# Folding query and key weights over a block diagonal, with the small weights' copies and the first maxima moved in the start of an attention kernel

## The chip, the cores and the metric

The kernel runs on one core of a Trainium2 chip. The metric is the device time of one execution in microseconds (us), the median of several runs. Engines are named as in the profile: PE (TensorE, matmuls; PEld its weight loads), ACT (ScalarE), DVE (VectorE), POOL (GpSimd), SP (the queue that issues DMAs). Each engine works through its own list of instructions strictly in the written order, and the lists meet only at semaphores.

## What is computed

For eight sequences of 1024 tokens and width 256, a layer norm feeds causal attention with 16 heads over a shared latent of 64, and a chain of three square weights with a tanh; both are added to the input.

```
xn      = layernorm(x)                         # x: 8 x 1024 x 256
q       = xn @ Wq                              # 16 heads of 64
latent  = xn @ Wkv_down                        # 64 wide, shared by all heads
k, v    = latent @ Wk_up, latent @ Wv_up
attn    = softmax(causal(q k^T / sqrt(64)))
y       = (attn @ v) @ Wout
ff      = tanh(xn @ weight @ aux1 @ aux2 + bias)
out     = x + y + ff
```

Since `k` is `latent @ Wk_up`, the kernel multiplies per head `Wq` by the transpose of `Wk_up` once ("folds" them) and never builds `k`; it does the same with `Wv_up` and `Wout`, and with the three square weights.

## The kernel before

**Staging.** The program is one plan, a list of named items, and each engine's program walks that list and emits its own part of each item. The list has two parts. `first_plan` is written out by hand: constants, layer norm of the first sequence, the turning (transposing) and folding of all weights, the first keys and queries, and the maxima of the first unit. `body_plan` comes from a planner (class `Order`) with its own table of costs; it holds the whole attention loop of 8 sequences and doesn't read `first_plan`. In the hand-written part the order of the tuple list is the order on every engine, so moving an item moves it in the queues of all engines that have a part in it.

**Items of the first part.** `LN0`, `LN1`, `LN4` are the layer norm on DVE; `T` transposes `x` on PE (L1121) into `xT_hi` (ACT, L1250) and its residue `xT_lo` (item `TL`, DVE, L1416). `W` items are the work on weights (functions `fold_on_pe`, `fold_on_act`, `fold_on_dve`): "turn wq" and "turn wk" transpose `Wq` and `Wk_up` (PE L814) and ACT copies the results to SBUF (L869); "fold wqk 0" and "fold wqk 1" multiply them for one half of the 256 input rows each (PE L839), ACT writes the rounded part `wqk_hi` (L869) and DVE the residue `wqk_lo` (L930). "turn others" transposes `Wv_up`, `aux1` and `weight` (L814); "fold aux" and "fold wff" are products of square weights (L796), "fold wvo" and the end of "fold wff" fold the values with `Wout` (L805), and "split wvo" is the DVE's residues of these (L936, L941). `K0`, `K` make the keys' latent and `Q0`, `Q` the folded queries (both L969, three products per result); `KN` turns the latent (L1143). After `Q`, ACT writes `q_hi` in two instructions and `q_lo` in one (L1269, L1274), SP copies halves of `q_hi` by two DMAs (L1477, L1479), and DVE makes the residue (`QL`, L1427), of which `QD` copies a part by DMA (L1487). `MAX` is a product whose row maxima DVE takes (L1062, L1299). `MT` turns the eight maxima of a unit (L1075), ACT copies them, and a DMA puts them in a row of `q_lo`, which the first score product `ST` (L1026, L1029) waits for. A DVE maximum of the body is L1304.

**Order and waits.** In a product the PE program waits for its inputs and for its PSUM bank to be left (`bank_left`): of the eight banks the `P0` items (`T`, `K`, `KN`, `Q`) take 6, 0 and 1 in turn, and the maxima take 2, 3 and 4. The compiler emits each fp32 product as two passes, so the 16 products of one "fold wqk" show as 32 matmuls in the trace; transposes and products of rounded (fp32r) operands are one pass each. In "fold wqk" a product takes one head: the stationary operand is 64 rows of `wqT` and the moving one 64 columns of `wkT`. The heads of a pair lie in the upper and the lower 64 rows.

**Loads.** SP issues all loads at the start in the order `x` (two halves), `Wq`, `Wk_up`, `Wkv_down`, `Wv_up` and the rest.

## Time and profile before

| | |
|---|---|
| median of 3 runs | 1976.43 us (1972.88 to 1980.48) |
| profiled execution, device time | 1977.45 us |
| its span, first to last instruction | 1975.7 us |
| mean granted PE clock | 0.994 |
| busy: PE, DVE, POOL, ACT | 99%, 69%, 73%, 58% of the span |
| first score product (L1026) starts | 55.18 us |

The profile is of one execution on its one core. Of the 1975.7 us the hand-written part takes the first 55, and the planner's body the rest. The chain that ended last is 89% PE; the largest shares of it are the products of the attention loop (L1044 23%, L969 21%, L1062 14%). To read the start, the timeline is of more use than the shares: it lists runs of equal instructions with their start and how long they lasted together. The granted clock (PEclk) is a share of full speed, with 1.00 for 2.4 GHz and 0.50 for 1.2 GHz.

### The profile page before, as it was taken

The page shows a single profiled execution, that of the slowest core. Times are in us where ns is not written, and L with a number is a line of the kernel's source. Part 1 is how long each engine was busy: PE and PEld are TensorE (multiplying, and loading weights), DVE is VectorE, ACT ScalarE, POOL GpSimd, SP SyncE. Part 2 cuts the span into 40 slices and gives each one's busy share as a digit, 9 for nine tenths or more (in the row PEclk, how much of TensorE's full clock was granted, in tenths as well). Part 3 has the DMA queues.
Part 4 walks back from the last instruction along what each step waited for, and adds up shares of the span by engine and source line. Part 5 has one row for each costly group of instructions (what it writes and reads, how often), then busy time and mean ns, then how long its engine had stood idle before and what let it go on. Part 6 is the DMA issues. An engine that isn't in the chain of part 4 may idle for free.

```text
span 1975.7 us, 38820 instructions
## 1 busy us (share of the span) xinstructions
PE 1948.6 (99%) x13568; PEld 1322.7 (67%) x13568; DVE 1372.7 (69%) x3623; ACT 1148.9 (58%) x2203; POOL 1450.7 (73%) x1276
## 2 busy tenths in 40 slices
PE   9999999999999999999999999999999999999997
PEld 7666666667666666766666666766676766766754
DVE  4778666786577867677676875868667786676642
ACT  4565565565566665656565565555665655655652
POOL 0577678886877867877778876877768777787882
PEclk8999999999999999999999999999999999999999
DMA  3222121212222212122122222122221221212210
GB/s 111 71 66 57 47 61 47 80 52 52 55 60 76 63 42 60 52 80 53 44 62 62 71 61 52 45 62 67 60 70 48 75 51 47 66 49 55 60 42 20
DMA packets 117599, 116.50 MB, mean 59 GB/s; under 512 B 24092, under 2 KB 100764, under 8 KB 117404
## 3 DMA queue, kind: packets, MB, share of 16 engines
q1 hardware_dynamic: 117404, 114.02, 21.7%
q8 instruction: 108, 1.77, 0.4%
q14 instruction: 87, 0.71, 0.1%
HBM read 53.67 MB, written 8.91 MB: 32 GB/s over the span
## 4 chain that ended last, share of the span: by engine, by line
PE 89%; DVE 4%; issue 3%; ACT 2%; POOL 1%; DMA 1%; POOLq 0%; ACTq 0%; SPq 0%; DVEq 0%
PE ps L1044 23%; PE ps L969 21%; PE ps L1062 14%; PE ps L1026 13%; PE ps L1029 12%; PE ps L1089 3%; DVE split_lo L1339 2%; POOL p_sum L1464 1%; PE ps L1075 1%; PE ps L1121 1%; DMA q_hi<-q_hi 1%; ACT probs L1199 1%; PE ps L839 0%; ACT q_hi L1269 0%; PE ps L1002 0%
## 5 line engine op out<-in xcount | busy, mean ns | idle before, releaser
L1464 POOL TENSOR_TENSOR p_sum<-p_sum,probs 128x512 f32<-128x512 f32 x660 | 845.9, 1309 | 132.0 <-ACT probs L1199 130.7
L1199 ACT ACTIVATE probs<-ps 128x512 f32<-128x512 f32 x1152 | 662.9, 598 | 308.6 <-PE ps L1029 292.2
L1299 DVE CUSTOM_DVE_ANT_0 ps<-ps,causal 128x512 f32<-128x512 f32 (+4 forms) x1024 | 520.1, 527 | 228.8 <-PE ps L1062 221.8
L1044 PE MATMUL ps<-probs,latent 128*32 128x512 f32 x4608 | 516.2, 594 | 0.0
L1062 PE MATMUL ps<-k_hilo,q_hi 128*128 128x512 f32 (+4 forms) x1536 | 471.3, 356 | 3.7 <-DMA q_hi<-q_hi 1.7
L1026 PE MATMUL ps<-q_hi,k_hilo 128*128 128x512 f32 x1152 | 470.1, 408 | 4.9 <-DVE wff_lo L936 1.9
L1029 PE MATMUL ps<-q_lo,k_ones 65*128 65x512 f32 x1152 | 457.1, 397 | 0.0
L1304 DVE TENSOR_REDUCE maxima<-ps 128x1 f32<-128x512 f32 (+1 forms) x512 | 326.2, 637 | 165.0 <-PE ps L1062 161.4
L1464 POOL TENSOR_TENSOR p_sum<-probs 128x512 f32<-128x512 f32 x222 | 288.7, 1318 | 128.2 <-ACT probs L1199 122.9
L1044 PEld LDWEIGHTS ps<-probs,latent 128*32 128x32 f32 x4608 | 139.7, 110 | 316.9 <-issue 312.2
L1062 PEld LDWEIGHTS ps<-k_hilo,q_hi 128*128 128x128 f32 x1536 | 279.3, 189 | 100.2 <-issue 25.5
L1450 POOL TENSOR_SCALAR_AFFINE_SELECT probs<-probs 128x512 f32<-128x512 f32 x256 | 166.8, 667 | 211.8 <-ACT probs L1199 211.2
L1026 PEld LDWEIGHTS ps<-q_hi,k_hilo 128*128 128x128 f32 x1152 | 217.9, 189 | 58.6 <-ACT probs L1199 28.5
L1029 PEld LDWEIGHTS ps<-q_lo,k_ones 65*128 65x128 f32 x1152 | 217.9, 189 | 18.1
L1208 ACT ACTIVATE y<-ps 128x512 f32<-128x512 f32 x128 | 76.5, 598 | 261.0 <-PE ps L1044 260.5
L1339 DVE TENSOR_TENSOR split_lo<-y,split_hi 128x512 fp32r<-128x512 f32 x127 | 171.1, 1348 | 49.0 <-ACT split_hi L1236 48.2
L1439 POOL TENSOR_TENSOR y<-y,norm 128x512 f32<-128x512 f32 x127 | 163.5, 1290 | 29.9 <-DMA norm<-recips 29.9
L1269 ACT ACTIVATE q_hi<-ps 64x512 fp32r<-64x512 f32 x256 | 151.6, 592 | 48.3 <-PE ps L969 45.4
L969 PE MATMUL ps<-wvo_hi,split_hi 128*128 128x256 f32 x512 | 150.1, 293 | 8.7 <-DVE split_lo L1339 7.6
L969 PE MATMUL ps<-xT_hi,wqk_hi 128*128 128x256 f32 x512 | 145.8, 285 | 0.0
L969 PE MATMUL ps<-wvo_lo,split_hi 128*128 128x256 f32 x512 | 145.3, 284 | 0.0
L969 PE MATMUL ps<-wvo_hi,split_lo 128*128 128x256 f32 x512 | 145.2, 284 | 0.0
(108 smaller groups left out, 2270.8 us busy)
## 6 DMA issues: line engine op xcount, KB each, us to landing
q_hi<-q_hi SPq DMA_DIRECT2D x256, 128.0 KB, 2.4
norm<-recips SPq DMA_DIRECT2D x254, 128.0 KB, 3.0
q_lo<-q_lo SPq DMA_DIRECT2D x128, 128.0 KB, 2.4
x_in<-in_L_attn_x_bld SPq DMA_DIRECT2D x16, 512.0 KB, 5.0
acc<-in_L_attn_x_bld SPq DMA_DIRECT2D x32, 256.0 KB, 3.1
out_x<-acc SPq DMA_DIRECT2D x64, 128.0 KB, 1.7
q_lo<-rows SPq DMA_DIRECT2D x128, 4.0 KB
rows<-norm SPq DMA_DIRECT2D x127, 4.0 KB
```

The lines of the kernel that those rows point to most:

```text
L969: last = nc.tensor.matmul(dst, weights(a, c), moving(b, c), start=(c == 0 and n == 0), stop=(c == of - 1 and n == 2))
L1026: nc.tensor.matmul(bank, k_hilo[par][:, blk], q_hi[buf][:, g:OCTET:2, columns(unit)], start=True, stop=False)
L1029: nc.tensor.matmul(bank, k_ones[par][:, blk], q_lo[buf][0:LATENT + 1, g:OCTET:2, columns(unit)], start=False, stop=True).then_inc(st_full, 1)
L1044: last = nc.tensor.matmul(y_bank[row:row + WIDTH, :], latent[par][:, key_block(unit, s), half:half + WIDTH], probs[:, t % PT_SLOTS, g * BA ...
L1062: nc.tensor.matmul(bank[:, 0:w], q_hi[half % Q_BUFS][:, h, columns(unit)], k_hilo[par][:, k0:k0 + w], start=True, stop=True).then_inc(max_ ...
L1199: nc.scalar.activation(probs[:, t % PT_SLOTS, g * BANK:(g + 1) * BANK], ps[:, bank_of[kind, key], :], ACT.Exp).then_inc(exp_done, 1)
L1299: nc.vector.tensor_tensor_reduce(bank, bank, causal[:, BANK - w:BANK], 1.0, LOWEST, ALU.add, ALU.max, maxima[:, unit % 4, h, 0:1]).then_in ...
L1304: nc.vector.tensor_reduce(maxima[:, unit % 4, h, 1:2], bank, AX.X, ALU.max).then_inc(max_free, 1)
L1339: nc.vector.tensor_tensor(split_lo[:, slot, :], y[:, key % Y_SLOTS, :], split_hi[:, slot, :].bitcast(F32), ALU.subtract).then_inc(norm_lo, 1)
L1439: nc.gpsimd.tensor_tensor(y[:, slot, :], y[:, slot, :], norm[:, slot, :], ALU.mult).then_inc(y_normal, 1)
L1450: nc.gpsimd.affine_select(out=v, in_=v, pattern=[[0, 4], [1, P]], compare_op=ALU.is_ge, fill=0.0, base=0, channel_multiplier=-1).then_inc( ...
L1464: nc.gpsimd.tensor_tensor(sums, other, probs[:, slot, part], ALU.add).then_inc(pool_done, 1)
```

## The change

Five things change, all of them in the hand-written first part.

1. "turn wk" comes ahead of "turn wq", and `Wk_up` is loaded ahead of `Wq`. ACT copies the turned key weights in two instructions of 64 rows into `wk_pairs`, in which a pair of heads is a 128x128 block with its two 64x64 blocks on the diagonal. POOL zeroes that tile first (an eighth constant), and ACT waits for it.
2. "fold wqk" takes a pair of heads in one product: 128 rows of `wqT` against the 128 columns of a block. It is 8 products of 128 columns instead of 16 of 64 in each item. In the first item PE waits for the copies of `wqT` bank by bank.
3. The copies of "turn others" go from ACT to DVE; `weight` is turned into bank 2 instead of 1, and with that the wait for bank 1 goes.
4. `KN` and the second `QL` and `QD` move behind "turn others", and the maxima stand ahead of and between the foldings in another split (2, 3 and 3, with banks 4, 3, 2 in turn).
5. `MT` comes ahead of the next queries, and "split wvo" right behind it.

```
-    plan += [("LN4", (0, k)) for k in range(2)] + [("W", "turn wq"), ("W", "turn wk")]
+    plan += [("LN4", (0, k)) for k in range(2)] + [("W", "turn wk"), ("W", "turn wq")]
...
-    plan += [*two_parts("Q", (0, 0)), ("QL", (0, 0)), *two_parts("Q", (0, 1)), ("KN", 0), ("QD", (0, 0))]
+    plan += [*two_parts("Q", (0, 0)), ("QL", (0, 0)), *two_parts("Q", (0, 1)), ("QD", (0, 0))]
...
-    plan += [("W", "turn others"), ("W", "fold aux"), *maxima[:2], ("QL", (0, 1)), ("QD", (0, 1)), maxima[2]]
-    plan += [("W", "fold wvo"), *maxima[3:6], ("W", "fold wff"), *maxima[6:]]
-    plan += [("Q0", (1, 0)), ("MT", 0), ("Q", (1, 0)), *two_parts("Q", (1, 1))]
+    plan += [("W", "turn others"), ("KN", 0), ("QL", (0, 1)), ("QD", (0, 1)), *maxima[:2]]
+    plan += [("W", "fold aux"), *maxima[2:5], ("W", "fold wvo"), *maxima[5:], ("W", "fold wff")]
+    plan += [("MT", 0), ("W", "split wvo"), *two_parts("Q", (1, 0)), *two_parts("Q", (1, 1))]
     plan += [("QL", (1, 0)), ("QD", (1, 0)), ("XA", 0), ("XA", 1), ("XA", 2)]
-    plan += [("W", "split wvo"), ("QL", (1, 1)), ("QD", (1, 1))]
+    plan += [("QL", (1, 1)), ("QD", (1, 1))]
...
-            bank[kind, key] = 2 + n_max % 3
+            bank[kind, key] = 4 - n_max % 3
...
-        wkT = acc_flat[:, 0:512].rearrange("p (j n) -> p j n", n=LATENT)
+
+        wk_pairs = probs[:, 8, :].rearrange("p (j n) -> p j n", n=2 * LATENT)
...
+                (wk_in, Wk_up.rearrange("c h k -> c (h k)"), wk_loaded),
                 (wq_in, Wq.rearrange("(c p) h k -> p c (h k)", p=P), wq_loaded),
-                (wk_in, Wk_up.rearrange("c h k -> c (h k)"), wk_loaded),
...
+            nc.gpsimd.memset(probs[:, 8, :], 0.0).then_inc(consts_made, 1)
...
-                for g in range(2):
-                    r = g * HD
-                    for j in range(HEADS // 2):
-                        last = nc.tensor.matmul(
-                            wq_banks[2 * c + g][:, j * LATENT:(j + 1) * LATENT],
-                            wqT[r:r + HD, j, c * P:(c + 1) * P], wkT[r:r + HD, j, :],
-                            start=True, stop=True)
-                    last.then_inc(w_full, 1)
+                for j in range(HEADS // 2):
+                    if c == 0 and j % 2 == 0:
+                        pe.wait_ge(w_copied, 3 + j // 2)
+                    last = nc.tensor.matmul(wq_banks[2 * c + j // 4][:, j % 4 * P:(j % 4 + 1) * P],
+                                            wqT[:, j, c * P:(c + 1) * P], wk_pairs[:, j, :],
+                                            start=True, stop=True)
+                    if j % 4 == 3:
+                        last.then_inc(w_full, 1)
             elif what == "turn others":
-                bank_left(1)
...
-                for bank, w in ((7, aux1_in), (1, w_in)):
+                for bank, w in ((7, aux1_in), (2, w_in)):
...
-                pe.wait_ge(w_copied, 12)
+                pe.wait_ge(w_turned, 3)
...
-                copied(5, acc_flat[:, 0:512], wk_bank)
+                act.wait_ge(consts_made, 8)
+                pairs = wk_bank.rearrange("p (j n) -> p j n", n=LATENT)
+                for g in range(2):
+                    rows = slice(g * HD, (g + 1) * HD)
+                    copied(1, wk_pairs[rows, :, g * LATENT:(g + 1) * LATENT], pairs[rows, :, :])
...
-            elif what == "turn others":
-                copied(10, acc_flat[:, 512:1024], ps[:, 5, :])
-                copied(11, norm[:, 0, :], ps[:, 7, :])
-                copied(12, acc_flat[:, 1536:2048], ps[:, 1, :])
...
+            elif what == "turn others":
+                for n, (dst, bank) in enumerate(((acc_flat[:, 512:1024], 5), (norm[:, 0, :], 7),
+                                                 (acc_flat[:, 1536:2048], 2))):
+                    dve.wait_ge(w_full, 10 + n)
+                    nc.vector.tensor_copy(dst, ps[:, bank, :]).then_inc(w_turned, 1)
```

What that makes of the engines' lists is shown at three places; names are the program's buffers, sizes are those of the moving operand or the output, and a line number of the changed kernel is a few higher for the same statement. The brackets name the semaphores waited for ahead of an instruction.

ACT at its start, before: the table load, the copies of the turned weights (`probs<-ps`), of `x` (`xT_hi`) and of the folded weights (`wqk_hi`).

```order
L869 ACT_TABLE_LOAD
L869 ACTIVATE probs<-ps 128x512 [waits w_full] x5
L1250 ACTIVATE xT_hi<-ps 128x512 [waits p0_full] x2
L869 ACTIVATE wqk_hi<-ps 128x8x64 [waits w_full] x2
L1250 ACTIVATE xT_hi<-ps 128x512 [waits p0_full] x2
```

ACT at the same place with the change.

```order
L872 ACT_TABLE_LOAD [waits w_full]
L872 ACTIVATE probs<-ps 64x8x64 [waits consts_made]
L872 ACTIVATE probs<-ps 64x8x64 [waits w_full]
L872 ACTIVATE probs<-ps 128x512 [waits w_full] x4
L1257 ACTIVATE xT_hi<-ps 128x512 [waits p0_full] x2
L872 ACTIVATE wqk_hi<-ps 128x512 [waits w_full] x2
```

The two half-height copies of the key weights stand ahead of the four of `wqT`, and the table load, which carried no wait before, stands behind a wait for the first turned weights (`w_full`).

PE from the end of the first queries to the second fold of the values, before: `k_hilo` with `ident` is `KN`, `p_sum` and `y` are the small weights to be turned, `y,norm` is "fold aux", `k_hilo,q_hi` a maximum's product and `probs` of 64x256 "fold wvo".

```order
L1143 MATMUL ps<-ident,k_hilo 128x64 [waits p0_free]
L1143 MATMUL ps<-ident,k_hilo 128x64 x7
L814 MATMUL ps<-ident,p_sum 128x64 [waits others_loaded,kn_copied]
L814 MATMUL ps<-ident,p_sum 128x64 x7
L814 MATMUL ps<-ident,y 128x128 x8
L796 MATMUL ps<-y,norm 128x256 [waits p0_free,w_copied]
L796 MATMUL ps<-y,norm 128x256 x3
L1062 MATMUL ps<-k_hilo,q_hi 128x512 [waits q_twice0_0]
L1062 MATMUL ps<-k_hilo,q_hi 128x512 x2
L805 MATMUL ps<-probs 64x256 [waits w_copied]
L805 MATMUL ps<-probs 64x256 x11
L1062 MATMUL ps<-k_hilo,q_hi 128x512 [waits max_free]
```

PE at the same place with the change.

```order
L817 MATMUL ps<-ident,p_sum 128x64 [waits others_loaded]
L817 MATMUL ps<-ident,p_sum 128x64 x7
L817 MATMUL ps<-ident,y 128x128 x8
L1150 MATMUL ps<-ident,k_hilo 128x64 [waits p0_free]
L1150 MATMUL ps<-ident,k_hilo 128x64 x7
L1069 MATMUL ps<-k_hilo,q_hi 128x512 [waits q_twice0_0]
L1069 MATMUL ps<-k_hilo,q_hi 128x512
L799 MATMUL ps<-y,norm 128x256 [waits p0_free,w_turned]
L799 MATMUL ps<-y,norm 128x256 x3
L1069 MATMUL ps<-k_hilo,q_hi 128x512
L1069 MATMUL ps<-k_hilo,q_hi 128x512 [waits max_free]
L1069 MATMUL ps<-k_hilo,q_hi 128x512 [waits max_free,q_twice0_1]
```

`KN` has moved behind the turning, whose wait for `kn_copied` is gone; two maxima stand ahead of "fold aux", which waits for `w_turned` in place of `w_copied`.

DVE ahead of the first score product, before: maxima (`ISA`), the residue of the next queries (`q_lo`), then the residues of the folded weights.

```order
L1299 ISA ps,maxima<-ps,causal 128x512 [waits max_full]
L1299 ISA maxima 128x1
L1427 TENSOR_TENSOR q_lo<-ps,q_lo 128x2x256 [waits p0_hi]
L936 TENSOR_TENSOR wff_lo<-ps,wff_hi 128x512 [waits w_copied]
L941 TENSOR_TENSOR wvo_lo<-ps,wvo_hi 128x512 [waits w_copied]
L941 TENSOR_TENSOR wvo_lo<-ps,wvo_hi 128x512 x3
L1427 TENSOR_TENSOR q_lo<-ps,q_lo 128x2x256 [waits p0_hi]
L1304 TENSOR_REDUCE maxima<-ps 128x1 [waits max_full]
```

DVE at the same place with the change.

```order
L1306 ISA ps,maxima<-ps,causal 128x512 [waits max_full]
L1306 ISA maxima 128x1
L943 TENSOR_TENSOR wff_lo<-ps,wff_hi 128x512 [waits w_copied]
L948 TENSOR_TENSOR wvo_lo<-ps,wvo_hi 128x512 [waits w_copied]
L948 TENSOR_TENSOR wvo_lo<-ps,wvo_hi 128x512 x3
L1434 TENSOR_TENSOR q_lo<-ps,q_lo 128x2x256 [waits p0_hi] x2
L1311 TENSOR_REDUCE maxima<-ps 128x1 [waits max_full]
L1306 ISA ps,maxima<-ps,causal 128x320 [waits max_full]
```

Both residues of the next queries now stand behind the five of the folded weights.

## Rows read from the trace of the kernel before

**Rows 1.** Busy time by stretch of the span; columns as in the answer's first line.
```profile
core 0: us, PE busy (x) PEld busy (x) DVE busy (x) ACT busy (x) POOL busy (x), PEclk, DMA share, GB/s
0.00:13.50 13.50, 11.69 (x48) 7.55 (x48) 9.77 (x42) 4.09 (x7) 1.93 (x11) 1.00 0.88 264
13.50:17.70 4.20, 4.20 (x40) 4.12 (x40) 3.10 (x9) 2.14 (x5) 0.00 (x0) 0.97 0.84 264
17.70:27.60 9.90, 9.90 (x43) 8.77 (x42) 3.28 (x5) 2.48 (x5) 0.00 (x0) 0.50 0.00 0
27.60:34.50 6.90, 5.04 (x38) 4.70 (x36) 2.08 (x3) 5.87 (x11) 0.00 (x0) 0.99 0.16 38
34.50:41.30 6.80, 6.09 (x23) 5.02 (x24) 0.00 (x0) 1.79 (x3) 0.00 (x0) 0.50 0.25 58
...
100.00:1900.00 1800.00, 1792.77 (x12566) 1219.38 (x12565) 1289.23 (x3398) 1070.92 (x2058) 1384.78 (x1208) 1.00 0.22 59
```

**Rows 2.** Timeline, 0 to 20 us: start us, us, engine, line, what.
```profile
0.80 1.28 ACT L869 ACT_TABLE_LOAD   x1 [0.80 <-PEq L1592]
...
9.51 1.91 PE L814 MATMUL ps<-ident,probs 128*128 128x128 f32 x16
...
10.14 2.56 ACT L869 ACTIVATE probs<-ps 128x512 f32<-128x512 f32 x5 [8.06 <-PE ps L814]
...
11.35 0.71 PE L814 MATMUL ps<-ident,p_sum 64*128 64x64 f32 x8
...
12.49 1.09 PE L1121 MATMUL ps<-ident,x_in 128*128 128x128 f32 x8 [0.43 <-DVE x_in L1404]
...
13.51 3.39 PE L839 MATMUL ps<-probs 64*128 64x64 f32 x32
13.88 1.29 DVE L1416 TENSOR_TENSOR xT_lo<-ps,xT_hi 128x512 fp32r<-128x512 f32 x2 [0.15 <-ACT xT_hi L1250]
...
15.47 0.49 DVE L923 TENSOR_TENSOR wkv_lo<-norm,wkv_hi 128x128 fp32r<-128x128 f32 x2
...
18.21 6.29 PE L839 MATMUL ps<-probs 64*128 64x64 f32 x32
```

**Rows 3.** Timeline, 24 to 33 us.
```profile
24.43 0.79 PE L969 MATMUL ps<-xT_hi,wkv_hi 128*128 128x512 f32 x1
...
28.32 0.40 PE L969 MATMUL ps<-xT_lo,wkv_hi 128*128 128x512 f32 x1
...
28.78 0.28 PE L969 MATMUL ps<-xT_hi,wqk_hi 128*128 128x256 f32 x1
...
31.66 0.98 PE L1143 MATMUL ps<-ident,k_hilo 128*128 128x64 f32 x8
...
32.38 0.62 SPq L1479 DMA_DIRECT2D q_hi<-q_hi  x1
```

**Rows 4.** Chain that ended last, in time order, 38 to 58 us.
```profile
38.22 3.51 PE ps L796 x8
41.73 0.68 PE ps L1062 x3
42.42 2.81 PE ps L805 x24
...
46.12 1.73 PE ps L796 x8
...
50.87 0.27 PE ps L1075
...
57.42 0.60 DVE q_lo L1427
```

**Rows 5.** Timeline, 51 to 56 us.
```profile
51.89 1.20 ACT L1269 ACTIVATE q_hi<-ps 64x512 fp32r<-64x512 f32 x2 [0.45 <-PE ps L969]
...
54.81 0.60 ACT L1274 ACTIVATE q_lo<-ps 128x512 fp32r<-128x512 f32 x1
```

**Rows 6.** DMA issues of the first 60 us: KB each, us to landing.
```profile
probs<-in_L_attn_Wq SPq DMA_DIRECT2D x1, 1024.0 KB, 7.5
...
q_hi<-q_hi SPq DMA_DIRECT2D x8, 128.0 KB, 2.4
```

More of the change, by code:

```diff
@@ L670, in build @@
         w_split = sem("w_split")
+        w_turned = sem("w_turned")
         x_loaded = [sem(f"x_loaded{i}") for i in range(2)]
@@ L823, in fold_on_pe @@
             elif what == "turn wq":
-                pe.wait_ge(consts_made, 7)
                 pe.wait_ge(wq_loaded, 16)
@@ L829, in fold_on_pe @@
             elif what == "turn wk":
+                pe.wait_ge(consts_made, 7)
                 pe.wait_ge(wk_loaded, 16)
@@ L832, in fold_on_pe @@
             elif what in ("fold wqk 0", "fold wqk 1"):
-                pe.wait_ge(w_copied, 5)
                 c = int(what[-1])
-                for g in range(2):
-                    r = g * HD
-                    for j in range(HEADS // 2):
-                        last = nc.tensor.matmul(
-                            wq_banks[2 * c + g][:, j * LATENT:(j + 1) * LATENT],
-                            wqT[r:r + HD, j, c * P:(c + 1) * P], wkT[r:r + HD, j, :],
-                            start=True, stop=True)
-                    last.then_inc(w_full, 1)
+                for j in range(HEADS // 2):
[6 more added lines that the diff above has]
+                        last.then_inc(w_full, 1)
             elif what == "turn others":
-                bank_left(1)
                 pe.wait_ge(others_loaded, 96)
                 transposes(ps[:, 5, :], [wv_in[:, j * P:(j + 1) * P] for j in range(HEADS // 2)])
-                for bank, w in ((7, aux1_in), (1, w_in)):
+                for bank, w in ((7, aux1_in), (2, w_in)):
                     transposes(ps[:, bank, :], [w[:, c, k * P:(k + 1) * P]
@@ L855, in fold_on_pe @@
             elif what == "fold wvo":
-                pe.wait_ge(w_copied, 13)
                 for n, bank in enumerate((5, 7, 6)):
+                    if bank == 6:
+                        pe.wait_ge(w_copied, 11)
                     wvo_bank(bank, n)
@@ L862, in fold_on_pe @@
                 square(0, wT, aux12)
+                bank_left(1)
                 wvo_bank(1, 3)
@@ L873, in fold_on_act @@
                 for n in range(4):
-                    copied(n + 1, wqT_flat[:, n * BANK:(n + 1) * BANK], wq_banks[n])
+                    copied(n + 2, wqT_flat[:, n * BANK:(n + 1) * BANK], wq_banks[n])
             elif what == "turn wk":
-                copied(5, acc_flat[:, 0:512], wk_bank)
+                act.wait_ge(consts_made, 8)
[3 more added lines that the diff above has]
+                    copied(1, wk_pairs[rows, :, g * LATENT:(g + 1) * LATENT], pairs[rows, :, :])
             elif what in ("fold wqk 0", "fold wqk 1"):
@@ L894, in wqk_part @@
         def wqk_part(w, n):
-            return (w[:, n // 2, :].rearrange("p (j g n) -> p j g n", g=2, n=LATENT)
-                    [:, :, n % 2, :], wq_banks[n].rearrange("p (j n) -> p j n", n=LATENT))
+            return w[:, n // 2, n % 2 * BANK:(n % 2 + 1) * BANK], wq_banks[n]
         def wvo_part(w, n):
@@ L928, in fold_on_dve @@
                     lo, bank = wqk_part(wqk_lo, n)
-                    dve.wait_ge(w_copied, 6 + n)
+                    dve.wait_ge(w_copied, 7 + n)
                     nc.vector.scalar_tensor_tensor(
@@ L933, in fold_on_dve @@
                         op1=ALU.subtract).then_inc(w_split, 1)
+            elif what == "turn others":
[3 more added lines that the diff above has]
+                    nc.vector.tensor_copy(dst, ps[:, bank, :]).then_inc(w_turned, 1)
             elif what == "split wvo":
-                dve.wait_ge(w_copied, 17)
+                dve.wait_ge(w_copied, 15)
                 nc.vector.tensor_tensor(wff_lo[:, :, :].rearrange("p c n -> p (c n)"), ps[:, 0, :],
@@ L938, in fold_on_dve @@
                                         ALU.subtract).then_inc(w_split, 1)
-                dve.wait_ge(w_copied, 18)
+                dve.wait_ge(w_copied, 16)
                 for n, bank in ((3, 1), (0, 5), (1, 7), (2, 6)):
```

## The prediction

> **What bounds the kernel now.** I read the busy time by stretch first. From 100 to 1900 us PE is busy for 1792.77 of 1800 us at full clock [rows 1], so the body is one queue of PE work, and what comes late into it comes out late by as much. The body's lists are the same in both kernels. So the question is how much earlier the start hands over. In the start I then read clock and idle time by stretch: PE stands at half clock from 17.7 to 27.6 and from 34.5 to 41.3 us, and idles for 1.9 of the 6.9 us between them [rows 1]. Then the timeline, for what each step waits for: the first transposes of x come at 12.49 behind DVE's normalization; the two foldings take 3.39 us at full and 6.29 us at half clock [rows 2]; the keys begin at 24.43 [rows 3]. Last the chain in order of time: fold aux 3.51 us, the other foldings and the maxima one behind another, MT at 50.87, and DVE's residue of the second next queries ending at 58.02 [rows 4]. That last end is my finish line, since the body's maxima queue behind it on DVE and PE needs their banks; behind it PE has no more long gaps.
>
> **The start up to the keys.** The clock and the warm-up are as before. PE turns the key weights at 9.5 in 0.7 us, then Wq in 1.9 us, to 12.1 [rows 2]. Wq landed 7.5 us after its issue, at 9.3 [rows 6]. It is now issued one DMA later (some 0.6 us, as the issue in [rows 3]) behind 0.25 MB, which at the 264 GB/s of the stretch is 1.0 us [rows 1], so it lands between 9.9 and 10.3. x's transposes still start at 12.5, at worst 12.7.
>
> ACT has a new cost. Before, the table load ran at 0.80 for 1.28 us while ACT had nothing to do [rows 2]. In the changed list it stands behind the wait for the first turned weights. It now runs from 10.3 to 11.6. Then come six copies instead of five at a pitch of 0.49 us (2.56 us for five, the last lasting 0.60) [rows 2], to 14.7, and the two of x to 15.2 and 15.7. DVE's residue of x, at 13.88 before, starts at 15.3. From there DVE has two residues (1.3 us), the casts and their residues (0.8 us, from the end of the first two to 15.96), two of the folded weights and two more of x, each about 0.65: 4.7 us, to 20.1 [rows 2]. The keys wait for the last of these and start at 20.2.
>
> Here the Trainium skill's page "ScalarE: Activation LUTs", section "What ACT_TABLE_LOAD costs", speaks against the change: it puts a load at about 1.28 us and a drain of some 1.38 us behind it. The row agrees with the first figure and can't show the second, as nothing followed. With 2.66 us the keys would start at 21.5, and the gain below would be 12.2 us, an estimate from that page.
>
> On PE a pair product is two passes with 128 columns moving and a 128x128 load. None such is in the trace. From below, the transposes of the same size run at 0.12 us each (1.91 for 16); from above, two-pass products with 256 columns (fold wff, 1.73 for 8) take 0.22 [rows 2, 4]. I take 0.12, as the columns streamed are the transposes'. Each folding is then 16 x 0.12 = 1.9 us: 13.6 to 15.5, x's other transposes to 16.5, the second folding to 18.4. The four waits of the first folding cost nothing: the copies end at 13.2, 13.7, 14.2 and 14.7, each before its pair is due. So PE is done at 18.4 and DVE sets the keys' start: 20.2 against 24.43, a gain of 4.2 us. POOL's added memset I cost at nothing: all of POOL's eleven instructions at the start take 1.93 us [rows 1], and even one as long as these together would end before ACT needs the tile at 11.6.
>
> **The clock.** The granted clock fell to 0.50 after the narrow foldings, whose passes have 64 rows loaded and 64 columns moving, and again after a stretch with 1.9 us of idle PE [rows 1, 2]. Both causes shrink: the new foldings load and stream twice as much per pass, and the idle time in the second place goes. I expect full clock throughout. The keys (12 x 0.23) and queries (24 x 0.12, both pitches from [rows 3]) then take 5.7 us instead of 7.2, to 25.9: a gain of 1.5 us.
>
> **From the queries to MT.** Before, PE waited after KN for ACT, which had six query copies and latent in front, turned at half clock, waited for ACT's copies, and folded aux at half clock. From 31.66 to 50.87 is 19.2 us [rows 3, 4]. Now the turning follows the queries directly: 0.7 for the values and 0.95 for eight of 128 columns, to 27.6; KN 1.0, to 28.5. The first two maxima need q_hi's DMAs: the first queries end at 24.5, ACT's two copies at 25.8, the second DMA is issued 0.7 later (as 32.38 is behind the first) and lands in 2.4 [rows 3, 6], at 29.0. So 0.5 us of wait; the two products take 0.5, to 29.5. Beside this DVE copies the three banks. Its copy of 128x512 is not in the trace; between 0.3 (half of a residue, which reads two operands) and 0.65 us I take 0.65, as the nearest row is its residues from PSUM [rows 2]. From 27.1 they end at 29.1, under the maxima; by the lower bound they end earlier and nothing is gained. Then PE works without a pause: fold aux 1.8, three maxima 0.7, fold wvo 2.8, three maxima 0.9, fold wff 1.75, its last bank 0.95 (a third of 2.81) [rows 4]. That is 8.9 us, and MT comes at 38.4. DVE's maxima, eight at 0.65 from 29.7, run inside the foldings; before, two of them stood alone ahead of MT. 12.5 us instead of 19.2: a gain of 6.7 us.
>
> **From MT to the body.** Before, 50.87 to 58.02, 7.15 us: DVE's five residues of the foldings stood between those of the two queries. Now they run from 38.4 to about 42, under the queries and their copies. PE's first half of the queries ends at 40.1, ACT's six copies take 3.5 (51.89 to 55.41) [rows 5], to 43.7, and the residue 0.7, to 44.4. MT's row needs ACT and a DMA, by q_hi's rows 0.7 to issue and 2.4 to land [rows 3, 6], so the first score products may start at 42.0 and don't set the end. 6.0 instead of 7.15: a gain of 1.15 us. What is late next is ACT, with the query copies.
>
> **The sum.** 4.2 + 1.5 + 6.7 + 1.15 = 13.6 us (58.02 to 44.4). Off the profiled execution's own 1977.45 us that is 1963.9. That execution is 1.0 above the median of the runs, so off the median it is 1962.8. I say 1963.0, 0.7% faster.
>
> **Rivals.**
> One half-clock stretch stays. PE's idle time of 1.8 us at 18.4 to 20.2 and the narrow work behind the queries speak for it. A stretch like that of 34.5 to 41.3, 6.8 us long, costs 3.4 us: a gain of 10.2 and 1966.2. Against it, the idle time lies between dense products, and the body, which has waits too, runs at 1.00 from 100 to 1900 us [rows 1]. The Trainium skill's "TensorE: Matmul & The Clock Gate", Part 4, says that transposes don't count as busy for the clock; 16 of them with KN and a wait behind would be such a place. Here the clock stayed at 1.00 through 9.5 to 13.5 us, which is nearly all transposes [rows 1, 2], so I give it 12%.
>
> Dear pair products. If a pass takes 0.22 as in fold wff, each folding takes 3.5 us, PE is the later one before the keys at 21.6, and the gain is 12.2: 1964.3. Against it, where load and stream are 128 each, as in the transposes, the load is hidden. 8%.
>
> The table load costs nothing. If it ran early or were hidden, DVE's residues of x would start at 13.9 as before and the keys at 18.7: a gain of 15.1 or 1961.3. Its place in the list speaks against it. 10%.
>
> The change does not do what it says: the start is shorter, and the body gives it back, since some later wait hangs on a transfer or a pace that the start does not move. About 1976. For it: PE's 7 us of idle time in the body. Against it: these are waits for other engines whose work moves with PE's. 7%.
>
> Slower. The clock, once half in the start, stays so into the body. From 20.2 to 44.4 us PE has about 20 us of work. At half clock all of it would add 20, less 13.6 gained: 1983. It decides from 13.6 us of full-clock work done at half, that is 27 us at half clock, against the 16.7 that the rows of before show in two pieces. With smaller mishaps of that sign, 4%.
>
> **How the numbers follow.** The forecast's own case has the rest, 59%. Unknown costs in it: the copies and the products' pace (up to 2 us lost), the table load's tail (1.4 lost), Wq's landing (0.2), better packing by 1 us, and the spread of before's runs, which is 4 us either way and 1 or 2 for a median. That is 1959 to 1968, and with the rivals near it 1958.5 to 1969 holds eight in ten. This kernel's measurement can tell about 0.5%, 9.9 us, from no change, which is at 1966.5. Faster by over that: 59 + 10 + 8 and half of the 12%, less a little for spread: 0.81. Within: 0.15. Slower: 0.04.
>
> **What would show it.** In the changed profile: ACT_TABLE_LOAD at about 10.3 for 1.28 us; each folding 16 passes in 1.9 us; DVE's residues of x as the releaser of the keys at 20.2; a granted clock of 1.00 from 13.5 to 44; no idle PE before the turning; MT near 38.4; the first score product near 42 against 55.18; and the body at its old pace, ending 13 to 14 us earlier. The prediction is wrong if the keys start after 22, if a half-clock stretch is left, or if a body event that came a given time after the first score product comes later after it now.

## The result and the profile after

The changed kernel takes 1964.13 us (median of 6 runs, 1960.96 to 1969.53) against 1978.45 for the kernel before in the same measurement (6 runs, 1972.88 to 1981.56). The medians are 14.3 us apart. The ratio is 0.994 with a 95% interval of 0.992 to 0.9959, which is 12 us of 1978 with an interval of 8 to 16: faster, clear of the noise. The profiled execution's span is 1962.0 us against 1975.7, 13.7 us less; 13.6 was forecast for this difference.

The busy time by stretch, for comparison with [rows 1]:

```profile
core 0: us, PE busy (x) PEld busy (x) DVE busy (x) ACT busy (x) POOL busy (x), PEclk, DMA share, GB/s
0.00:13.50 13.50, 10.84 (x42) 6.83 (x43) 9.66 (x40) 3.20 (x5) 2.83 (x12) 1.00 0.88 238
13.50:17.70 4.20, 4.20 (x40) 4.20 (x39) 3.32 (x11) 4.20 (x9) 0.00 (x0) 1.00 1.07 338
17.70:27.60 9.90, 8.73 (x67) 7.89 (x65) 6.05 (x11) 6.52 (x13) 0.00 (x0) 1.00 0.07 17
27.60:34.50 6.90, 6.40 (x44) 4.57 (x43) 5.21 (x13) 2.74 (x5) 0.00 (x0) 1.00 0.42 97
34.50:41.30 6.80, 6.80 (x47) 5.50 (x46) 5.02 (x11) 3.18 (x7) 0.00 (x0) 1.00 0.01 3
...
100.00:1900.00 1800.00, 1793.87 (x12578) 1220.00 (x12577) 1293.25 (x3391) 1073.06 (x2061) 1388.35 (x1212) 1.00 0.22 59
```

In 17.7 to 27.6 and 34.5 to 41.3 us, where PE stood at 0.50 before, it now runs at 1.00. The body is unchanged: PE is busy for 1793.87 of 1800 us against 1792.77. Measured from PE's restart behind the last residue of the queries (58.47 us before, 44.72 now; called the gate below) to the end of the span it lasts 1917.2 us before and 1917.3 now. In these two executions the start's 13.75 us arrive whole at the end. The line of the chain from which the gate before is read:

```profile
58.47 0.56 PE ps L1062 x2
```

That the two bodies agree to 0.1 us is chance, though. The experiments below have the same body, and in their profiled executions it lasts from 1914.2 us (MT as before) to 1921.4 us (zeros by ACT): from 100 to 500 us PE was busy for 399.20 us in the first of these and for 395.06 in the second. So a trace shows exactly what the start gains, but the time of one execution shows it only to within some 7 us.

The start's timeline, which answers to [rows 2] and the first row of [rows 3]:

```profile
2.85 0.95 POOL L790 MEMSET probs<- 128x1024 f32 x1
2.93 0.91 DVE L911 CAST ident<-norm 128x64 fp32r<-128x64 f32 x1 [2.93 <-POOL causal L786]
...
10.24 1.28 ACT L872 ACT_TABLE_LOAD   x1 [10.24 <-PE ps L817]
...
11.44 1.97 PE L817 MATMUL ps<-ident,probs 128*128 128x128 f32 x16 [1.28 <-DMA probs<-in_L_attn_Wq]
11.54 3.31 ACT L872 ACTIVATE probs<-ps 64x512 f32<-64x512 f32 x6
...
13.28 1.09 PE L1128 MATMUL ps<-ident,x_in 128*128 128x128 f32 x8
...
14.21 1.95 PE L841 MATMUL ps<-probs 128*128 128x128 f32 x16
...
15.36 1.29 DVE L1423 TENSOR_TENSOR xT_lo<-ps,xT_hi 128x512 fp32r<-128x512 f32 x2 [0.84 <-ACT xT_hi L1257]
...
16.87 1.95 PE L841 MATMUL ps<-probs 128*128 128x128 f32 x16
...
19.99 0.47 PE L976 MATMUL ps<-xT_hi,wkv_hi 128*128 128x512 f32 x1 [1.17 <-DVE xT_lo L1423]
```

The table load stands at 10.24 where it was at 0.80, and ACT's six copies end at 14.85. The foldings take 1.95 us each where they took 3.39 and 6.29. DVE's residue of x starts at 15.36, and the keys wait for it until 19.99. PE also idles 1.28 us for Wq ahead of 11.44, where the kernel before shows no wait for it.

The chain in time order, which answers to [rows 4] (start, us, engine, what):

```profile
28.81 0.74 PE ps L1069 x2
29.55 1.73 PE ps L799 x8
...
31.98 2.74 PE ps L808 x24
...
38.34 0.21 PE ps L1082
...
43.58 0.69 DVE q_lo L1434
...
44.72 0.55 PE ps L1069 x2
```

From the first maxima at 28.81 PE works without a pause to MT at 38.34, with fold aux in 1.73 us where it took 3.51. The timeline, which shows an instruction's own start, has MT at 38.27 and the first score product at 41.26, where it stood at 55.18:

```profile
41.26 0.40 PE L1033 MATMUL ps<-q_hi,k_hilo 128*128 128x512 f32 x1
```

In the text and the table below MT is read from the timeline and the gate from the chain.

### The profile page after: what moved, and what is told of

Its sections match the earlier page's. It is cut to its first block, busy times and chain, and to the rows that moved or that the text cites. A ratio compares the mean times of both kernels' runs of the same rounds, so it can differ in the third digit from the quotient of the medians.

```text
span 1962.0 us, 38758 instructions
## 1 busy us (share of the span) xinstructions
PE 1938.4 (99%) x13536; PEld 1315.6 (67%) x13536; DVE 1379.7 (70%) x3626; ACT 1146.9 (58%) x2201; POOL 1451.3 (74%) x1277
## 4 chain that ended last, share of the span: by engine, by line
PE 90%; DVE 4%; issue 3%; ACT 2%; POOL 1%; DMA 0%; ACTq 0%; POOLq 0%; SPq 0%; DVEq 0%
PE ps L1051 22%; PE ps L976 22%; PE ps L1069 14%; PE ps L1033 14%; PE ps L1036 13%; DVE split_lo L1346 3%; PE ps L1096 3%; POOL p_sum L1471 1%; PE ps L1082 1%; ACT probs L1206 1%; PE ps L1128 1%; PE ps L824 0%; PE ps L1009 0%; ACT q_hi L1276 0%; PE ps L1150 0%
## 5 line engine op out<-in xcount | busy, mean ns | idle before, releaser
L1069 PEld LDWEIGHTS ps<-k_hilo,q_hi 128*128 128x128 f32 x1536 | 279.2, 189 | 98.1 <-issue 24.7
L976 PE MATMUL ps<-wvo_hi,split_hi 128*128 128x256 f32 x512 | 151.1, 295 | 10.3 <-DVE split_lo L1346 9.2
```

Source lines behind the costliest of these rows:

```text
L976: last = nc.tensor.matmul(dst, weights(a, c), moving(b, c), start=(c == 0 and n == 0), stop=(c == of - 1 and n == 2))
L1069: nc.tensor.matmul(bank[:, 0:w], q_hi[half % Q_BUFS][:, h, columns(unit)], k_hilo[par][:, k0:k0 + w], start=True, stop=True).then_inc(max_ ...
```

## The experiments

Each line gives the start of the keys, MT on PE, and the gate, all read from the one profiled execution of each kernel, and the ratio to the kernel before on the same chip with its 95% interval.

| kernel | keys | MT | gate | median us (runs) | ratio |
|---|---|---|---|---|---|
| before | 24.43 | 50.87 | 58.47 | 1975.4 (56) | 1 |
| changed | 19.99 | 38.27 | 44.72 | 1964.13 (6) | 0.994 [0.992, 0.9959] |
| narrow folds, the rest changed | 26.55 | 46.04 | 52.49 | 1969.47 (12) | 0.9972 [0.9957, 0.9987] |
| pairs only, old copies and order | 19.71 | 42.68 | 50.30 | 1967.48 (12) | 0.9963 [0.995, 0.9976] |
| MT and last residues as before | 19.60 | 38.70 | 46.30 | 1964.06 (4) | 0.9943 [0.992, 0.9965] |
| copies on ACT as before | 19.71 | 38.20 | 44.65 | 1962.92 (4) | 0.9941 [0.9918, 0.9964] |
| table load early | 19.05 | 37.35 | 43.79 | 1960.5 (4) | 0.9932 [0.9908, 0.9956] |
| Wq first | 19.05 | 37.35 | 43.80 | 1960.9 (6) | 0.9927 [0.9906, 0.9947] |
| Wq first, zeros by ACT | 18.39 | 36.69 | 43.13 | 1962.04 (6) | 0.993 [0.9909, 0.9951] |
| Wq first, folds of 64 rows x 64 columns | 27.03 | 48.0 | 54.44 | 1972.78 (12) | 0.9968 [0.9947, 0.9989] |
| Wq first, folds of 128 rows x 64 columns | 22.05 | 40.2 | 46.61 | 1966.14 (11) | 0.9946 [0.9928, 0.9964] |

The 56 runs of the kernel before are those beside the experiments, on three chips, where its medians were 1973.96, 1975.53 and 1976.69 us. So times of different lines are best compared by the ratio.

**Narrow folds in the changed kernel.** The products' shape is undone, and with it the wait bank by bank: the first product waits for all copies.

```
-                    last = nc.tensor.matmul(wq_banks[2 * c + j // 4][:, j % 4 * P:(j % 4 + 1) * P],
-                                            wqT[:, j, c * P:(c + 1) * P], wk_pairs[:, j, :],
+                for g in range(2):
+                    r = g * HD
+                    for j in range(HEADS // 2):
+                        last = nc.tensor.matmul(
+                            wq_banks[2 * c + g][:, j * LATENT:(j + 1) * LATENT],
+                            wqT[r:r + HD, j, c * P:(c + 1) * P],
+                            wk_pairs[r:r + HD, j, r:r + LATENT], start=True, stop=True)
```

> The changed kernel with only the shape of the folding products put back: 16 products per item of 64 rows and 64 columns instead of 8 of 128 and 128, everything else (table load, copies, maxima, MT) as changed. My theory: the narrow products are what let the granted clock fall at 17.5 us in the kernel before. Then each folding takes 3.4 us at full clock, the second one runs at half clock (about 6 us), the keys start at 24 to 25 instead of 20.0 and run at half clock for some 3 us: the body's gate (44.7 in the changed kernel) comes 5.5 to 7 us later and the time is about 1970. Rival: the clock fell for the idle time around the transposes, not for the products. Then it stays at 1.00 here, both foldings take 3.4, the keys start near 22.2, and the time is about 1966.

The gate came 7.8 us later than in the changed kernel, where my theory had 5.5 to 7, and the keys at 26.55 instead of 24 to 25; the median was 1969.5, as expected. Busy time by stretch, columns as above:

```profile
8.00:12.50 4.50, 2.96 (x24) 2.28 (x23) 4.02 (x25) 3.01 (x5) 0.00 (x0) 0.95 1.06 296
12.50:15.20 2.70, 2.70 (x14) 2.37 (x12) 1.93 (x7) 2.21 (x5) 0.00 (x0) 0.50 1.10 348
...
18.90:29.00 10.10, 10.10 (x46) 9.17 (x45) 3.46 (x5) 2.79 (x5) 0.00 (x0) 0.50 0.00 0
```

The clock fell twice. The long stretch, 18.9 to 29.0, covers the second folding and the keys as before. The short one, about 12.1 to 15.5, is new: it begins behind the 1.54 us in which PE waited for Wq in this execution. It is one reason why keys and gate came later than the theory had them. So this kernel does not separate the shape of the products from the idle time ahead of them; the last two experiments do.

**Pairs only.** The small weights' copies go back to ACT, and the items to the old order.

```
-    plan += [("W", "turn others"), ("KN", 0), ("QL", (0, 1)), ("QD", (0, 1)), *maxima[:2]]
-    plan += [("W", "fold aux"), *maxima[2:5], ("W", "fold wvo"), *maxima[5:], ("W", "fold wff")]
-    plan += [("MT", 0), ("W", "split wvo"), *two_parts("Q", (1, 0)), *two_parts("Q", (1, 1))]
+    plan += [("W", "turn others"), ("W", "fold aux"), *maxima[:2], ("QL", (0, 1)), ("QD", (0, 1)), maxima[2]]
+    plan += [("W", "fold wvo"), *maxima[3:6], ("W", "fold wff"), *maxima[6:]]
+    plan += [("Q0", (1, 0)), ("MT", 0), ("Q", (1, 0)), *two_parts("Q", (1, 1))]
```

> The changed kernel with pair products, key weights turned first and the late table load, but with the small weights copied by ACT again and KN, maxima, MT and the last residues in the order of before. My theory: the queries end at 25.7 as in the changed kernel (5.9 us earlier than before), and from there the old 19.2 us to MT and 7.6 to the body's gate come back, with the half clock around fold aux: MT at 44.5 to 45, gate at 52.5, time about 1971 to 1972. Rival: with the first half-clock stretch gone the second goes too, and the order gains nothing by itself beyond its waits: MT at 42, gate at 49, time about 1968.

Busy time by stretch, columns as before:

```profile
17.70:28.00 10.30, 9.16 (x68) 8.20 (x67) 5.14 (x9) 7.09 (x13) 0.00 (x0) 1.00 0.12 27
28.00:30.80 2.80, 0.93 (x4) 0.74 (x4) 0.00 (x0) 1.76 (x4) 0.00 (x0) 0.90 0.64 145
30.80:33.70 2.90, 2.90 (x9) 2.28 (x8) 0.00 (x0) 0.20 (x1) 0.00 (x0) 0.51 0.00 0
...
47.00:51.00 4.00, 4.00 (x14) 3.39 (x15) 3.31 (x7) 1.41 (x3) 1.27 (x2) 0.57 0.55 124
```

MT came at 42.7, between what the two theories gave. PE stood for 1.88 us, to 29.93, while ACT worked off its queries, latent and copies. Behind that the clock fell, for some 3 us instead of the 6.8 before, and fold aux took 3.52 us again; the turning ahead of it ran at full clock this time. It fell once more at about 47.3, ahead of this kernel's gate. So the old order has half-clock stretches of its own, shorter here than I had taken from the one trace of before. Pairs alone move the gate by 8.2 us, which leaves 5.6 of the 13.75 for the copies and the order. That these add up is no test; what tests it is the kernel of narrow folds, where undoing the pairs alone cost 7.8. By the times, 0.9963 and 0.9972 make 0.9935 together, and 0.994 was measured for both.

**MT and the last residues as before.**

```
-    plan += [("MT", 0), ("W", "split wvo"), *two_parts("Q", (1, 0)), *two_parts("Q", (1, 1))]
+    plan += [("Q0", (1, 0)), ("MT", 0), ("Q", (1, 0)), *two_parts("Q", (1, 1))]
...
-    plan += [("QL", (1, 1)), ("QD", (1, 1))]
+    plan += [("W", "split wvo"), ("QL", (1, 1)), ("QD", (1, 1))]
```

> The changed kernel with only MT behind the first half of the next queries and the residues of the foldings (split wvo) between those of the queries, as before. My theory: MT comes 0.7 us later (39.0) and DVE's last query residue is held by five residues, so the distance from MT to the body's gate is 7.6 us again instead of 6.4: gate at 46.6 instead of 44.7, and a time near 1966. Rival: this order costs nothing since ACT's six copies end at 43.6 either way, and the gate stays at 44.7 to 45.

Its chain in time order:

```profile
38.87 0.11 PE ps L1082
...
42.86 2.39 DVE wvo_lo L948 x4
45.25 0.60 DVE q_lo L1434
...
46.30 0.90 PE ps L1069 x2
```

The timeline has MT at 38.70, so the gate at 46.30 is 7.6 us behind it, as expected, with DVE's four residues of the values (2.39 us) ahead of the query residue. The keys started 0.4 us earlier than in the changed kernel's trace, so the cost of the old order is 1.6 plus 0.4, 2.0 us. There is also a half-clock stretch from about 43.7 to 47.1, which the changed kernel's trace does not have. It is no part of these 2.0 us, since the chain to the gate runs on ACT and DVE from 39.7 on; it costs behind the gate, where the two maxima take 0.90 us and not 0.55. The 4 runs can't show either as time: their median is 1964.06, where I had expected 1966.

**Copies on ACT.**

```
-                    dve.wait_ge(w_full, 10 + n)
-                    nc.vector.tensor_copy(dst, ps[:, bank, :]).then_inc(w_turned, 1)
+                    act.wait_ge(w_full, 10 + n)
+                    nc.scalar.activation(dst, ps[:, bank, :], ACT.Copy).then_inc(w_turned, 1)
```

> The changed kernel with only the three small weights' copies on ACT again. My theory: with KN out of the way ACT is free at 27.9 us and copies by 29.5; fold aux, which waits for two maxima until 29.5 anyway, starts 0 to 0.3 us later, and the time is as the changed kernel's. Rival: ACT's latent copy and the next copies come late behind it, and fold aux starts at 30 or later with an idle PE and a half-clock stretch behind it: gate at 47 or later, time 1967.

The gate is at 44.65. From the keys' start it is 24.9 us, against 24.7 in the changed kernel: handing the copies to DVE is worth about 0.2 us once KN stands behind the turning, by one trace of each. What the old copies cost before was their place in ACT's queue, behind latent, as the kernel with pairs only shows.

**Table load early.** A one-element copy at ACT's start.

```
+            act.wait_ge(consts_made, 1)
+            nc.scalar.activation(early[:, :], causal[0:1, 0:1], ACT.Copy)
```

> The changed kernel with a one-element copy at ACT's start, so that the table load runs at 0.8 us; loads and memset as changed. If the table load is what delays x's residue, it starts at 14.6 instead of 15.4 (then Wq's landing at 11.3 and the turning behind it set the transposes of x at 13.3) and the keys start at 19.2 instead of 20.0. If the six copies behind it set it, the keys stay at 20.0. Either way under 1 us of 1964, no difference in the time.

Its timeline on ACT:

```profile
0.80 1.28 ACT L1191 ACT_TABLE_LOAD   x1 [0.80 <-PEq L1602]
...
2.10 0.20 ACT L1191 ACTIVATE early<-causal 1x1 f32<-1x1 f32 x1
```

The load is back at 0.80, and the keys start at 19.05, 0.94 us earlier, about as expected. Not all of it is the table load: in this execution Wq landed 8.0 us after its issue instead of 8.9, and DVE, which in the changed kernel's trace had waited 0.27 us for the second half of x, began to normalize at 11.61 instead of 11.84. That accounts for about 0.2 us. It also shows how long ACT is held: the next instruction starts at 2.10, 1.30 us after the load began. In the changed kernel the first copy starts 1.30 us behind the load's start as well (10.24 to 11.54).

**Wq first.** The loads and the turning in the old order, pairs kept.

```
-    plan += [("LN4", (0, k)) for k in range(2)] + [("W", "turn wk"), ("W", "turn wq")]
+    plan += [("LN4", (0, k)) for k in range(2)] + [("W", "turn wq"), ("W", "turn wk")]
...
-                    if c == 0 and j % 2 == 0:
-                        pe.wait_ge(w_copied, 3 + j // 2)
+                    if c == 0 and j == 0:
+                        pe.wait_ge(w_copied, 6)
```

> The changed kernel with only Wq loaded and turned ahead of the key weights again. That also frees the table load, since ACT's first copy then carries no second wait. My theory: the wait for Wq (9.4 to 11.4 us) and the late table load are the two costs that the change brings; without both, the keys start near 19.1 instead of 20.0 (POOL's memset still delays DVE by 0.7 us), and the body's gate comes near 43.8. PE has no idle second ahead of x's transposes, so no half-clock stretch falls there: mean clock 0.997 or more in most runs, and a median of about 1962. Rival: the order of the loads is neutral for the clock, and the median stays at that of the changed kernel over before, a ratio of 0.994.

Its chain in time order:

```profile
14.43 1.29 DVE xT_lo L1423 x2
...
19.05 4.45 PE ps L976 x24
...
43.80 0.56 PE ps L1069 x2
```

Keys and gate came where expected, and level with the early table load: turning the key weights first buys nothing that these traces show and costs the table load's place. The ratio is 0.9927 against 0.994, with overlapping intervals. The mean granted clock of the 6 runs is 0.997, of the changed kernel's 0.996; 6 runs each don't settle whether the wait for Wq costs clock in a typical run.

**Wq first, zeros by ACT.** POOL's memset goes, and four copies of a zero tile on the idle ACT take its place.

```
-            nc.gpsimd.memset(probs[:, 8, :], 0.0).then_inc(consts_made, 1)
...
+            for at in range(0, 8 * P, 2 * P):
+                nc.scalar.activation(probs[:, 8, at:at + 2 * P], causal[:, 0:2 * P],
+                                     ACT.Copy).then_inc(w_zeroed, 1)
```

> The changed kernel with Wq loaded and turned first again, POOL's memset of the block tile replaced by four copies of zeros on ACT at its idle start, so that the table load runs at 0.8 us. My theory: table load and Wq's landing are what held x's residues; x's transposes start at 12.5 as in the kernel before, DVE's residue of x starts at 13.9 instead of 15.4, the keys start at 18.7 instead of 20.0, and the body's gate comes at 43.4 instead of 44.7: 1.3 us earlier, a time of about 1963, which the runs cannot tell from the changed kernel. Rival: ACT has six copies of weights ahead of x's, and its queue holds the residue of x to 14.4 or later whatever the table load does; then the keys start at 19.3 or later and at most 0.7 us is gained.

Its timeline:

```profile
2.93 0.20 DVE L911 CAST ident<-norm 128x64 fp32r<-128x64 f32 x1 [2.93 <-POOL causal L787]
...
18.39 0.47 PE L976 MATMUL ps<-xT_hi,wkv_hi 128*128 128x512 f32 x1 [0.47 <-DVE xT_lo L1427]
```

This is the shortest start of all: keys at 18.39 and gate at 43.13, 1.6 us ahead of the changed kernel. DVE's first cast is back at 0.20 us, and the keys gain the last 0.66 us over the kernel above. Its ratio, 0.993, beats the kernel before clearly and the changed one not measurably.

**Rows or short passes.** The first try cut each pair product in two columns' halves, on the changed kernel:

```
+                    for r in (0, HD):
+                        at = j % 4 * P + r
+                        last = nc.tensor.matmul(wq_banks[2 * c + j // 4][:, at:at + LATENT],
+                                                wqT[:, j, c * P:(c + 1) * P],
+                                                wk_pairs[:, j, r:r + LATENT],
```

> The changed kernel with each pair product cut into two of 128 rows and 64 columns (16 products per item, zeros multiplied as well). If the loads of 128 columns set the pace of a pass, the 32 passes take 0.10 to 0.12 us each, 3.4 us per folding, as the narrow ones did; if the 64 columns streamed set it, 0.06 us each and 1.9 us per folding. On the clock: if the fall needs few rows at work, the clock stays at 1.00 here although the passes are as short as the narrow ones; if short passes between loads are enough, it falls at about 17.5 as before and the keys start after 24.

The foldings took 3.52 us each, 0.11 us a pass, so the 64 columns streamed don't set the pace. What does is, by my first theory, the load of 128: in the trace of this shape below, loads are busy for 4.97 of 5.00 us. The clock was at 1.00 through them, but it had been at 0.50 from about 11.6 to 15.0 us, behind a wait of 1.79 us for Wq. Its one time was 1964.58 us. So I put both shapes on the kernel with Wq first, where that wait is small.

```
-                                            wqT[:, j, c * P:(c + 1) * P], wk_pairs[:, j, :],
+  64 rows:                                  wqT[r:r + HD, j, c * P:(c + 1) * P], wk_pairs[r:r + HD, j, r:r + LATENT],
+ 128 rows:                                  wqT[:, j, c * P:(c + 1) * P], wk_pairs[:, j, r:r + LATENT],
```

> Wq loaded and turned first (no second of idle PE ahead of x's transposes) and the foldings narrow, 64 rows and 64 columns, 16 products per item. Each folding is 32 passes in 3.4 us at full clock. If few rows at work are what lets the clock fall, it falls in the second folding at about 17.5 to 19, that folding takes 5 to 6 us, the keys start at 23 to 24.5 and the body's gate is 47.5 to 50; time near 1966 to 1968. If short passes behind loads of 128 columns are enough, this kernel and the next one show the same clock and the same times.

> The same kernel with products of 128 rows and 64 columns, also 16 per item, so that passes, loads and their count are the same as in the one above and only the rows at work differ. Each folding should again take 3.5 us at full clock. If the rows matter, the clock stays at 1.00, the keys start at 21.6 and the gate is near 46.3; time near 1963.5, 3 us under the other. If the shortness of the passes matters, the clock falls at 17.5 to 19 here too and both have the same time, near 1967.

In the 64-row kernel the results and their order are also those of before, all upper heads ahead of the lower ones.

64 rows, by stretch (columns as in the first fence: the third number from the end is the granted clock), and its chain:

```profile
13.00:18.00 5.00, 4.96 (x37) 4.80 (x38) 4.02 (x11) 2.33 (x5) 0.00 (x0) 0.77 0.92 291
18.00:23.00 5.00, 5.00 (x24) 4.55 (x23) 2.08 (x3) 1.79 (x3) 0.00 (x0) 0.50 0.00 1
...
28.00:33.00 5.00, 5.00 (x16) 4.03 (x15) 1.08 (x2) 1.59 (x4) 0.00 (x0) 0.52 0.00 0
```

```profile
14.13 4.77 PE ps L843 x32
...
20.80 6.22 PE ps L843 x32
27.03 7.08 PE ps L979 x24
...
54.44 0.56 PE ps L1072 x2
```

128 rows, the same:

```profile
13.00:18.00 5.00, 4.97 (x45) 4.97 (x46) 4.01 (x11) 2.31 (x5) 0.00 (x0) 1.00 0.82 257
18.00:23.00 5.00, 5.00 (x42) 4.83 (x41) 2.86 (x5) 2.47 (x5) 0.00 (x0) 1.00 0.00 0
...
28.00:33.00 5.00, 4.50 (x33) 4.02 (x31) 4.47 (x9) 2.40 (x5) 0.00 (x0) 1.00 0.65 151
```

```profile
14.13 3.52 PE ps L843 x32
...
18.52 3.52 PE ps L843 x32
22.05 4.25 PE ps L979 x24
...
46.61 0.56 PE ps L1072 x2
```

At full clock both shapes have the same pace (3.5 us per folding with 128 rows; 3.49 for the first folding of the narrow kernel above). With 64 rows the clock fell to 0.50 in the first folding, at about 15.7, and stayed there to about 32.8, through the other transposes, the second folding and the keys; with 128 rows it did not fall. The idle time ahead is alike, 0.95 and 0.67 us with 64 rows, 0.25 and 1.04 with 128; and with pair products on the same kernel ("Wq first") 0.81 and 0.94 us brought no fall. The gates are 7.8 us apart, and the medians 6.6 us (the means 4.6, with a standard error of 1.3). The difference has the sign that I expected of the rows, but about twice the size: I had the fall in the second folding and the gates 1.2 to 3.7 us apart, and 3 us between the times. The mean granted clock is 0.9942 against 0.9969 over the runs. Two runs of the 64-row kernel show 0.998 and 0.999 and took 1966.5 and 1962.9 us, so it seems that the fall doesn't come in every execution; of those two there is no trace.

## Why the prediction was right

**The body as a queue.** Right: 1917.2 and 1917.3 us from gate to end. But the body lasts 1914.2 to 1921.4 us in the traces of the experiments, so that the spans differ by 13.7 us, as forecast to 0.1, is luck as far as the last few microseconds go. By the prediction's own sign, a body event came 0.2 us later after the first score product than before (the gate 3.46 us behind it against 3.29), which is far inside that variation.

**Up to the keys: 20.2 forecast, 19.99 measured, by a sum in which two terms were wrong and hidden.** Table load at 10.24, six copies to 14.85, residue of x at 15.36 and keys at 19.99 are the chain as forecast. But Wq landed 8.9 us after its issue, at 11.3, where I had 9.9 to 10.3 from the stretch's 264 GB/s (8.0 to 8.6 us in the other executions with the key weights first); and x's transposes started at 13.28, not at 12.5 to 12.7. The latter I had put down to DVE alone and unchanged. In fact DVE was late from its first cast on, which took 0.91 us (0.20 in the kernel without POOL's memset). That put x's statistics 0.55 us back, and a wait of 0.27 us for x's second half came on top; PE, too, was turning Wq until about 13.3. POOL's memset, which I had costed at nothing because ACT needs it late, thus cost DVE 0.7 us where nothing else held it, and the keys 0.66 once the table load was out of the way. This and Wq's landing hid under the table load, and the memset showed once that was taken away: keys at 19.05 and not at the 18.7 that the prediction gave for that rival, and 18.39 with the memset gone as well.

**The foldings' pace: 0.12 us a pass.** Right, 1.95 us each.

**The clock.** Right for the profiled execution. For the first stretch the cause is now shown and not only argued: passes of the same number and pace with 64 and with 128 rows differ in it. For the second stretch the idle PE is not isolated; with pairs only, the clock fell again behind 1.88 us of it. The share that is the clock's is larger than the 1.5 us that the sum gave it, since the 6.29 us of the second folding was in the 4.2. Of the gate's 13.75 us, 7.8 went back with the narrow products alone, a part of that by the short stretch behind the wait for Wq.

**From the queries to MT: 12.5 forecast, 12.5 measured** (25.8 to 38.3), with 0.50 us of wait for q_hi's DMA as forecast. The step's attribution needs a correction. With pairs only and the old order it takes 17.3 us (25.4 to 42.68): so 1.9 of the 6.7 us come with the pairs, mostly in that the turning no longer runs at half clock, and 4.8 with the copies and the order. Of these the copies on DVE are worth 0.2; KN's place, the order of the maxima and the half-clock fold aux no run separates.

**From MT to the body: 6.0 forecast, 6.0 measured** (38.27 to 44.27), with ACT's query copies last, as forecast. The first score product came at 41.26, where I had 42.0, and set nothing. Undoing the step's change made it 7.15 us again (38.70 to 45.85), exactly what it was.

**The rivals.** No half-clock stretch was left in the start of the profiled execution. In other runs of the changed kernel there may be one, as their mean clocks go from 0.994 to 0.998 and their times from 1969.5 down to 1961.0. The Trainium skill's "ScalarE: Activation LUTs", section "What ACT_TABLE_LOAD costs", states a drain of about 1.38 us beside the load for every switch to a different set. It is not borne out here for a program's first load: the next instruction came 1.30 us after the load's start, at an idle start (0.80 to 2.10) and on the chain (10.24 to 11.54), and the keys started at 19.99 and not at the estimate's 21.5. Dear pair products did not occur (1.95 us a folding), and neither did the slower case or a body that gives the gain back.

**The median.** 1964.13 against 1963.0, and a gain of 14.3 against 13.6; by the ratio it is 12. The kernel before had medians of 1973.96 to 1978.45 us in different measurements, which is more than either miss. So the mechanism was right but for the two hidden terms, and the closeness of the last digit is luck.

## What to carry to other kernels

When a kernel's body is one saturated queue, look for gain in the idle and half-clock time ahead of it; it arrives at the end, though single executions of the body may differ by as much (here by 7 us). Compare the lists of waits of both kernels, not only the diff: a second wait ahead of the first activation moved a table load of 1.28 us from an idle start onto the path. A term costed at nothing because its consumer is late can still hold up the engine beside it.

## What the runs showed of the hardware

- The rows at work in a product bear on TensorE's clock. With the same number of passes at the same full-clock pace (0.11 us), the granted clock stood at 0.50 from 15.7 to 32.8 us with 64 rows, and at 1.00 throughout with 128; the mean over the runs was 0.9942 and 0.9969.
- The mean granted clock goes with most of the spread between runs: over the 56 runs of the kernel before, it ranges from 0.987 to 0.997 and correlates with the time by -0.91, with 1.5 us per 0.001. The 1988.35 us run is the one of 0.987, the 1969.08 one has 0.997.
- An idle PE of 1.5 to 1.8 us at the start, waiting for Wq, was followed by a half-clock stretch in the traces of two kernels (about 12.1 to 15.5 and 11.6 to 15.0). Behind the 1.28 us of the changed kernel's trace there was none. The length of the wait alone doesn't decide it: later, behind 1.88 us of waiting to 55.18 in the kernel before and 1.51 us to 44.72 in the changed one, the clock stayed at 1.00. No experiment isolates this.
- Transposes alone did not hold the clock down. In the first try of 128 rows by 64 columns PE ran nothing but transposes from 10.92 to 15.26, and the clock, at 0.50 since 11.6, was back at 1.00 from about 15.0 on.
- A cast of 128x64 on DVE, 0.20 us alone, took 0.91 us beside POOL's memset of 128x1024 (2.85 to 3.80) and ended 0.04 us after it.
- A pass of 64 columns behind a load of 128 takes 0.11 us and one of 128 columns 0.12 us, so a pair product of twice the columns is nearly free.
